# FFN stage: x plus its norm made by GpSimd from x alone, x (1 + rstd) - mean rstd, in one step with two per-row scalars (q's turn standing between k tile and q pair)

## The chip, the cores and the metric

The kernel runs on one core of a Trainium2 chip. The metric is the device time of one execution in microseconds (us). One execution was also recorded by the hardware profiler. The engines are TensorE (PE, with its weight loads as PEld), VectorE (DVE), ScalarE (ACT), GpSimd (POOL) and SyncE (SP, which issues DMAs here).

## The reference, cut to what matters

There are 16 blocks b of 128 rows by 1024 columns, float32. A cross attention makes the new x, and then the feed-forward part (FFN) follows:

```python
x = x + xattn(layernorm(x), ctx, ctx, ...)
h = layernorm(x)                 # (x - mean) / sqrt(var + 1e-5), over the 1024 columns
query  = h @ Wq.T                # 64 columns
scores = top 8 of 256 slots, softmax over them, weighted values, two small products -> aux_out
u      = log-variance term of h + sigmoid(gelu(h @ Wu1.T + bu1) @ Wu2.T + bu2)
gate   = sigmoid(gate_w1 * clip(u) + gate_bias)
x = x + (h + gate * aux_out)
```

The last line needs x + h. With rstd = 1/sqrt(var + eps) of a row, h = x rstd - mean rstd, so x + h = x (1 + rstd) - mean rstd.

## The kernel before, in words

All 16 blocks of x stay in SBUF as `X[:, b, :]` (`x_all` in the profile). No scheduler is at work: each engine has its own instruction stream, written out by hand as a loop over periods `b` with four quarters `i`, and the engines meet at counting semaphores (`wait_ge`). In periods 0 to 15 the attention of block b, b-1, b-2 and b-3 is interleaved: k tiles (`k_tile`), the q pair (`q_pair`), the turn of q (`q_turn`, between the k tile and the q pair), the context product (`g_part`), the output pair (`o_pair`), the turn of the output (`o_turn`).

FFN part 1 is a chain of 17 steps, `hidden_step(0)` to `hidden_step(16)`. Steps 0 to 7 stand in the quarters of periods 17 and 18, among the last attention work, the others behind them. In step b:

- ACT copies the turned block b+1 out of PSUM (`hT_high`, hT_hi), applies gelu to block b-1 (`unit_gelu`), makes the norm of block b+2 into one of two buffers (`h_scale`: `hbuf` from `X`), and sums the units of block b-1 (`unit_sum`). `o_copy` and `o_square` of the attention's last blocks stand between the steps.
- PE turns block b+1 (`h_transpose`, reads `hbuf`) and multiplies block b with the weights (`hidden_products`, 24 matmuls).
- DVE makes the low part of the turned block (`hT_low`), multiplies the gelu result by a row of weights (`unit_weights`: `units<-units,Wu`, both inputs in SBUF), and moves the products out of PSUM (`unit_bias`, `query_rows`).
- GpSimd adds the norm to x in place (`hidden_sum`: `X[b] = X[b] + hbuf`), which frees `hbuf` as far as GpSimd reads it. Its semaphore is `y_done`.

`h_scale(b)` writes `hbuf[:, b % 2, :]`. It waits for the norm's scalars (`nb2_done`), for PE to have turned block b-2 (`h_T`) and for GpSimd to have added block b-2 (`y_done`). The scalars come from `rstd2_pow(b)` on GpSimd, four small instructions on 128x1 tiles; `nb2` is -mean rstd. GpSimd's stream in periods 17 and 18 holds, in this order: `hidden_sum(0)`, the scaling of q for the last quarter, `rstd2_pow(13)`, `norm_scale(14)` (L977, L979, L981), `hidden_sum(1)` to `(3)`, `rstd2_pow(14)`, `hidden_sum(4)`, `norm_scale(15)`, `hidden_sum(5)` to `(7)`, `rstd2_pow(15)`, and then `hidden_sum(8)` to `(15)` with one other subtraction (L1062) in front of block 11. DVE uses the rstd of all blocks once, between its steps 7 and 8 (`varh`, L1330 and L1332, inputs in SBUF). `y_done` is also what part 2 waits for before it adds the gated term to `X[b]`.

FFN part 2 (from about 593 us) does the top 8, the softmax and the output products of the 16 blocks, and stores them.

Of the kernel before, what the change touches and what calls it, by code (L numbers as in the profile page):

```python
# [6 lines left out]
ALU = mybir.AluOpType  # L7
# [3 lines left out]
P = 128  # L11
B = 16
# [24 lines left out]
def wait(engine, sem, value):  # L37

    if value > 0:
        engine.wait_ge(sem, value)  # L40
# [7 lines left out]
def attention_ffn_kernel(nc, x, ctx_rows, ctx_cols, WqT_raw, WkT_raw, Wv_rows, WoT_rows, bo_row, g_col, Wuq_cols,  # L48
# [3 lines left out]
    with ctx:  # L52
        def sb(name, shape, dt=F32, scope=ctx):
            return scope.enter_context(nc.sbuf_tensor(name, shape, dt))

        def sem(name):
            return ctx.enter_context(nc.semaphore(name))


        X = sb("x_all", [P, B, N])  # L60
# [3 lines left out]
        mv2 = sb("mv2", [P, B, 2])  # L64
        rstd2 = sb("rstd2", [P, B, 1])
        nb2 = sb("nb2", [P, B, 1])
        VV = sb("VV", [P, NSLOT // P, P])
        scoreB = sb("scoreB", [P, 2 * NSLOT])

# [64 lines left out]
        hbuf = sb("hbuf", [P, 2, N], scope=ffn)  # L134
# [160 lines left out]
        ve2_done = sem("ve2_done")  # L295
        rstd2_done = sem("rstd2_done")
        mr2_done = sem("mr2_done")
        nb2_done = sem("nb2_done")

        wuq_hi = sem("wuq_hi")  # L300
# [9 lines left out]
        y_done = sem("y_done")  # L310
# [123 lines left out]
        def _(pe):  # L434
# [239 lines left out]
            def z_product(b, k):  # L674
                pe.wait_ge(wT_copied, b + 1)
                wait(pe, z_split, b)
                for s in range(NSLOT // P):
                    last = nc.tensor.matmul(z_psum, VV[:, s, :], wT[:, k, s, :], start=(s == 0),  # L678
                                            stop=(s == NSLOT // P - 1))
# [32 lines left out]
        def _(act):  # L712
# [64 lines left out]
            def h_scale(b, k):  # L777
                act.wait_ge(nb2_done, b + 1)
                wait(act, h_T, b - 1)
                wait(act, y_done, b - 1)  # L780
                nc.scalar.activation(hbuf[:, k, :], X[:, b, :], ACT.Identity, bias=nb2[:, b, :],
                                     scale=rstd2[:, b, :]).then_inc(h_done, 1)

# [14 lines left out]
            def hidden_step(b):  # L798
                if b + 1 < B:
                    hT_high(b + 1, (b + 1) % 2)  # L800
                if has(b - 1):
                    unit_gelu(b - 1, (b - 1) % 2)
                if b + 2 < B:
                    h_scale(b + 2, b % 2)
                if b == EARLY + 3:
                    act.wait_ge(varh_step, 2)
                    nc.scalar.activation(logv[:, :], varh[:, :], ACT.Ln, bias=ones[:, 0:1]).then_inc(logv_done, 1)
                if 0 < b < B:
                    unit_sum(b - 1, (b - 1) % 2)
# [14 lines left out]
            for b in range(PERIODS):  # L824
                p, o, e = b - 1, b - 2, b - 3
                for i in range(4):
# [6 lines left out]
                    if b == B + 1 and i == 0:  # L833
                        act.wait_ge(q_prod, 4 * B)
                        act.wait_ge(m_prod, B)
                        hT_high(0, 0)
                        h_scale(1, 1)
# [27 lines left out]
                    if b == 1 and i == 1:  # L865
                        act.wait_ge(vv_prod, NSLOT // P)
                        act.wait_ge(rk_prod, 1)
                        nc.scalar.copy(VV[:, :, :].rearrange("p s (r d) -> p s r d", d=VB),
                                       ob[:, 0:2 * VB].rearrange("p (s d) -> p s d", d=VB).unsqueeze(2).broadcast_to(
# [17 lines left out]
                    if b == B and i == 3:  # L887
                        for half in range(2):
                            act.wait_ge(k_moved[half], moved(B))
                        h_scale(0, 0)  # L890
# [49 lines left out]
        def _(pool):  # L940
# [43 lines left out]
            def rstd2_pow(b):  # L984
                pool.wait_ge(mv2_done, b + 1)
                nc.gpsimd.tensor_scalar(ve2[:, :], mv2[:, b, 1:2], LN_EPS, None, ALU.add).then_inc(ve2_done, 1)
                pool.wait_ge(ve2_done, b + 1)
                nc.gpsimd.tensor_tensor(rstd2[:, b, :], ve2[:, :], half_neg[:, 0:1], ALU.pow).then_inc(rstd2_done, 1)
                pool.wait_ge(rstd2_done, b + 1)
                nc.gpsimd.tensor_tensor(mr2[:, :], mv2[:, b, 0:1], rstd2[:, b, :], ALU.mult).then_inc(mr2_done, 1)  # L990
                pool.wait_ge(mr2_done, b + 1)
                nc.gpsimd.tensor_scalar(nb2[:, b, :], mr2[:, :], -1.0, None, ALU.mult).then_inc(nb2_done, 1)

            def hidden_sum(b):
                pool.wait_ge(h_done, b + 1)
                nc.gpsimd.tensor_tensor(X[:, b, :], X[:, b, :], hbuf[:, b % 2, :], ALU.add).then_inc(y_done, 1)

            nc.gpsimd.memset(half_neg[:, :], -0.5).then_inc(consts, 1)
            nc.gpsimd.memset(ones[:, :], 1.0).then_inc(consts, 1)
# [23 lines left out]
            for b in range(PERIODS):  # L1023
                p, o, e = b - 1, b - 2, b - 3
                for i in range(4):
                    if i == 0 and has(o):
                        mt_bias(o)
                    if i == 3 and 0 < b < B:
                        x_low(b)
                    if early_step(b, i) == 0:  # L1030
                        hidden_sum(0)
                    qb, qi = (p, i - 1) if i else (o, 3)
                    if has(qb):
                        q_scale(qb, qi)
                    if i == 0 and 0 < b < B:
                        rstd_pow(b)
                    if i == 0 and has(e - 1):
                        rstd2_pow(e - 1)
                    if i == 1 and b > 0 and has(b + 1):
                        ctx_low(b + 1)  # L1040
                    if i == 1 and has(e):
                        norm_scale(e)
                    if b == B and i == 3:
                        for half in range(2):
                            pool.wait_ge(k_moved[half], moved(B))
                        nc.gpsimd.memset(q_rows[:, :, BOT:P], 1.0).then_inc(query_ones, 1)
                    if early_step(b, i) > 0:
                        hidden_sum(early_step(b, i))
            rstd2_pow(B - 1)

            def output_scale(b):
# [6 lines left out]
            for b in range(EARLY, B):  # L1058
                hidden_sum(b)
                if b == EARLY + 2:  # L1060
                    pool.wait_ge(wvu_hi, 1)
                    nc.gpsimd.tensor_tensor(WvuT_lo[:, :], WvuT_in[:, :], WvuT_hi[:, :].bitcast(F32),  # L1062
                                            ALU.subtract).then_inc(wvu_lo, 1)
# [363 lines left out]
```

## Time and profile before

| | before |
|---|---|
| median of 3 runs | 643.58 us (642.69 to 644.58) |
| the profiled execution | 643.3 us |
| its span, first to last instruction | 641.4 us |
| mean granted TensorE clock | 0.997 of full speed |
| PE busy | 96% of the span |
| attention only, about 30.7 us a period | to about 500 us |
| steps of FFN part 1 | about 500 to 593 us |
| FFN part 2 | about 593 to 641 us |

The profiled execution lies 1.9 us over its span and 0.3 us under the median. "Busy" is the time in which an engine has an instruction running. Matmuls are pipelined: each row's duration reaches into the next one's, so the distance of two starts tells more than a duration.

### The profile page before, as it was taken

Reading aid. Unit: us, or ns where it says so; the run is one execution under the profiler, and the core shown is the slowest. Engines: PE = TensorE matmul, PEld = TensorE weight load, DVE = VectorE, ACT = ScalarE, POOL = GpSimd, SP = SyncE. Lnnn points to the kernel's source line nnn. Section 1 sums busy time; section 2 is a strip of 40 time slices with the busy share of each in tenths; the row PEclk is TensorE's granted clock in tenths of the full one; section 3 lists DMA queues with packets and bytes.
Section 4 is the critical chain, followed back from the end, with each engine's and each line's share of the span. In section 5 each row is a group of like instructions: output and inputs, shape, how many; then the busy total and the mean of one; then the engine's idle time right before and its main releaser. Section 6 shows DMA issues by size and latency. Waiting matters only on the chain.

```text
span 641.4 us, 11774 instructions
## 1 busy us (share of the span) xinstructions
PE 617.7 (96%) x3974; PEld 542.3 (85%) x3974; DVE 546.0 (85%) x757; ACT 416.7 (65%) x844; POOL 387.1 (60%) x353
## 2 busy tenths in 40 slices
PE   4899999999999999999999999999999989999896
PEld 3778888888888888888898888888888989988574
DVE  5989898988989898989898989898986745866896
ACT  5566766676676666667676766675665856674793
POOL 4954474747474747474747565665745668662394
PEclk9999999999999999999999999999999999999899
DMA  8933443444444444444445343443343100000056
GB/s 297 248 107 102 142 110 117 117 127 113 126 115 121 114 129 115 126 115 122 125 116 161 100 129 103 132 107 94 80 145 96 42 2 1 1 2 1 34 228 263
DMA packets 52010, 72.57 MB, mean 113 GB/s; under 512 B 10112, under 2 KB 42400, under 8 KB 51696
## 3 DMA queue, kind: packets, MB, share of 16 engines
q1 hardware_dynamic: 50912, 68.07, 36.3%
q0 software_dynamic: 896, 2.45, 1.2%
q10 hardware_dynamic: 144, 1.31, 0.6%
q8 instruction: 32, 0.52, 0.4%
q14 instruction: 26, 0.21, 0.1%
HBM read 29.85 MB, written 8.39 MB: 60 GB/s over the span
## 4 chain that ended last, share of the span: by engine, by line
PE 86%; DVE 4%; POOL 2%; ACT 2%; issue 2%; SPq 2%; DMA 1%; DVEq 0%; ACTq 0%
PE ob L502 17%; PE gm L479 17%; PE turn L463 8%; PE k_slot L437 5%; PE q_slot L437 5%; PE q_slot L439 4%; PE k_slot L439 4%; PE k_slot L438 4%; PE q_slot L438 4%; PE turn L554 3%; PE gm L488 2%; PE turn L510 2%; PE gm L554 2%; SPq L381 2%; PE turn L678 1%
## 5 line engine op out<-in xcount | busy, mean ns | idle before, releaser
L966 POOL TENSOR_TENSOR qs_sb<-qs_sb,qrec 128x1024 f32<-128x1024 f32 x64 | 122.0, 1906 | 151.2 <-DVE qrec L1131 151.2
L734 ACT ACTIVATE ek<-k_slot,nkm 128x1024 f32<-128x1024 f32 x62 | 69.1, 1114 | 95.5 <-DVE nkm L1096 95.4
L502 PE MATMUL ob<-mt_sb,q_hd 128*128 128x128 f32 x1024 | 126.4, 277 | 1.9 <-ACT o_sb L756 1.8
L502 PEld LDWEIGHTS ob<-mt_sb,q_hd 128*128 128x128 f32 x1024 | 121.8, 192 | 6.4 <-issue 4.8
L479 PE MATMUL gm<-ekT,ctxT 128*128 128x256 f32 x512 | 118.2, 379 | 0.9 <-DMA ekT<-kt 0.9
L479 PEld LDWEIGHTS gm<-ekT,ctxT 128*128 128x128 f32 x512 | 97.0, 190 | 15.9 <-DMA ekT<-kt 1.4
L744 ACT ACTIVATE qs_sb<-qs_sb 128x1024 f32<-128x1024 f32 x64 | 68.6, 1071 | 31.6 <-DVE qs_sb L1120 31.6
L1096 DVE TENSOR_REDUCE nkm<-k_slot 128x1 f32<-128x1024 f32 x62 | 74.2, 1197 | 16.1 <-PE k_slot L439 16.1
L1127 DVE TENSOR_REDUCE qsum<-qs_sb 128x16 f32<-128x1024 f32 x64 | 76.9, 1202 | 4.1 <-ACT qs_sb L744 4.1
L1120 DVE TENSOR_TENSOR qs_sb<-q_slot,qm 128x1024 f32<-128x1024 f32 x64 | 78.4, 1225 | 2.2
L1103 DVE STREAM_TRANSPOSE kt<-ek 128x1024 f32<-128x1024 f32 x64 | 78.5, 1227 | 0.0
L1117 DVE TENSOR_REDUCE qm<-q_slot 128x16 f32<-128x1024 f32 x64 | 75.5, 1180 | 0.0
L463 PE MATMUL turn<-ident,qs_sb 128*128 128x128 f32 x512 | 66.3, 272 | 0.0
L463 PEld LDWEIGHTS turn<-ident,qs_sb 128*128 128x128 f32 x512 | 59.6, 141 | 8.0 <-issue 0.5
L749 ACT COPY q_hd<-turn 128x1024 f32<-128x1024 f32 x64 | 64.3, 1005 | 2.9 <-PE turn L463 2.9
L437 PE MATMUL k_slot<-ctx_hi,WkT_hi 128*128 128x512 f32 x124 | 54.8, 442 | 9.5 <-DVE ctx_lo L1281 7.5
L437 PE MATMUL q_slot<-WqT_hi,xn_hi 128*128 128x512 f32 x128 | 55.7, 435 | 0.0
L439 PE MATMUL q_slot<-WqT_lo,xn_hi 128*128 128x512 f32 x128 | 50.6, 395 | 0.0
L438 PE MATMUL q_slot<-WqT_hi,xn_lo 128*128 128x512 f32 x128 | 49.8, 389 | 0.0
L439 PE MATMUL k_slot<-ctx_lo,WkT_hi 128*128 128x512 f32 x124 | 49.3, 398 | 0.0
L438 PE MATMUL k_slot<-ctx_hi,WkT_lo 128*128 128x512 f32 x124 | 49.0, 395 | 0.0
L960 POOL TENSOR_TENSOR xn_lo<-xn,xn_hi 128x1024 fp32r<-128x1024 f32 x16 | 38.3, 2392 | 14.9 <-ACT xn_hi L728 14.9
(199 smaller groups left out, 1250.8 us busy)
## 6 DMA issues: line engine op xcount, KB each, us to landing
ekT<-kt SPq DMA_DIRECT2D x496, 64.0 KB, 2.0
ctx_in<-ctx_rows SPq DMA_DIRECT2D x16, 512.0 KB, 4.6
x_all<-x SPq DMA_DIRECT2D x16, 512.0 KB, 3.5
ctxT<-ctx_cols SPq DMA_DIRECT2D x16, 512.0 KB, 4.1
out<-q_hd SPq DMA_DIRECT2D x15, 512.0 KB, 2.6
Wuq_in<-Wuq_cols ACTq DMA_DIRECT2D x1, 1280.0 KB, 6.3
x_all<-values_cols POOLq DMA_DIRECT2D x1, 1024.0 KB, 8.1
ekT<-kt POOLq DMA_DIRECT2D x16, 64.0 KB, 3.6
```

The source lines that it names most:

```text
L437: nc.tensor.matmul(dst, lhs[0], rhs[0], start=True, stop=False)
L438: nc.tensor.matmul(dst, lhs[1], rhs[0], start=False, stop=False)
L439: return nc.tensor.matmul(dst, lhs[0], rhs[1], start=False, stop=True)
L463: last = nc.tensor.transpose(turn[:, (2 * t + n) * P:(2 * t + n + 1) * P], qs_sb[:, i % 2, n * HALF + t * P:n * HALF + (t + 1) * P], ident ...
L479: last = nc.tensor.matmul(gm[:, cols], ctxT[:, b % 2, j, :], ekT[:, 2 * half:2 * half + 2, :, j * BLK:(j + 1) * BLK], start=(j == 0), stop ...
L502: last = nc.tensor.matmul(ob[:, (j % 4) * C:(j % 4 + 1) * C], q_hd[:, t, j * P:(j + 1) * P], mt_sb[:, b % 2, t, :], start=(t == 0), stop=( ...
L966: nc.gpsimd.tensor_tensor(e, e, qrec[:, i % 2, :].unsqueeze(2).broadcast_to([P, PAIR, DH]), ALU.mult).then_inc(q_mul, 1)
L1096: V.tensor_reduce(nkm[:, i:i + 1], k_psum(b, i)[:, :], AX, ALU.max, negate=True).then_inc(k_max, 1)
L1103: V.transpose(kt[:, i, :], ek[:, i % 2, :]).then_inc(k_T, 1)
L1117: V.tensor_reduce(qm[:, :], q, AX, ALU.max).then_inc(q_max, 1)
L1120: V.tensor_tensor(qs_sb[:, i % 2, :].rearrange("p (m d) -> p m d", d=DH), q, qm[:, :].unsqueeze(2).broadcast_to([P, PAIR, DH]), ALU.subtra ...
L1127: V.tensor_reduce(qsum[:, :], qs_sb[:, i % 2, :].rearrange("p (m d) -> p m d", d=DH), AX, ALU.add).then_inc(q_sum, 1)
```

## The change

Three things are edited. GpSimd's `hidden_sum` reads `X` alone and applies two per-row scalars, a multiply by `one_rstd2` and an add of `nb2`, in one instruction. The scalar `one_rstd2` = 1 + rstd is one further small GpSimd instruction in `rstd2_pow`. ACT's `h_scale` no longer waits for `y_done`. `hidden_sum(b)` still waits for `h_done`, since it overwrites `X[b]`, which `h_scale(b)` reads.

```diff
@@ h_scale (ACT) @@
                 act.wait_ge(nb2_done, b + 1)
                 wait(act, h_T, b - 1)
-                wait(act, y_done, b - 1)
                 nc.scalar.activation(hbuf[:, k, :], X[:, b, :], ACT.Identity, bias=nb2[:, b, :],
                                      scale=rstd2[:, b, :]).then_inc(h_done, 1)
@@ rstd2_pow and hidden_sum (GpSimd) @@
                 nc.gpsimd.tensor_scalar(nb2[:, b, :], mr2[:, :], -1.0, None, ALU.mult).then_inc(nb2_done, 1)
+                nc.gpsimd.tensor_scalar(one_rstd2[:, b, :], rstd2[:, b, :], 1.0, None, ALU.add).then_inc(one_rstd2_done, 1)
 
             def hidden_sum(b):
                 pool.wait_ge(h_done, b + 1)
-                nc.gpsimd.tensor_tensor(X[:, b, :], X[:, b, :], hbuf[:, b % 2, :], ALU.add).then_inc(y_done, 1)
+                pool.wait_ge(nb2_done, b + 1)
+                pool.wait_ge(one_rstd2_done, b + 1)
+                nc.gpsimd.tensor_scalar(X[:, b, :], X[:, b, :], one_rstd2[:, b, :], nb2[:, b, :], ALU.mult,
+                                        ALU.add).then_inc(y_done, 1)
```

GpSimd's stream in period 17, from `rstd2_pow(13)` to the start of `rstd2_pow(14)`, before (`rstd` and `nb` are rstd2 and nb2, names without their numbers):

```order
L992 TENSOR_SCALAR nb<-mr 128x1 [waits mr2_done]
L977 TENSOR_SCALAR l2c<-l 128x8 [waits l2_sum]
L979 TENSOR_TENSOR rn<-l2c,half_neg 128x8 [waits l2_clamped]
L981 TENSOR_TENSOR o_sb<-o_sb,rn 128x1024 [waits rn_pow]
L996 TENSOR_TENSOR x_all<-x_all,hbuf 128x1024 [waits h_done] x3
L986 TENSOR_SCALAR ve<-mv 128x1 [waits mv2_done]
```

and the same place of the changed kernel, whose lines have other numbers:

```order
L993 TENSOR_SCALAR nb<-mr 128x1 [waits mr2_done]
L994 TENSOR_SCALAR one_rstd<-rstd 128x1
L978 TENSOR_SCALAR l2c<-l 128x8 [waits l2_sum]
L980 TENSOR_TENSOR rn<-l2c,half_neg 128x8 [waits l2_clamped]
L982 TENSOR_TENSOR o_sb<-o_sb,rn 128x1024 [waits rn_pow]
L1001 TENSOR_SCALAR x_all<-x_all,one_rstd,nb 128x1024 [waits one_rstd2_done,nb2_done,h_done] x3
L987 TENSOR_SCALAR ve<-mv 128x1 [waits mv2_done]
```

Nothing changes its place: one small instruction is put in, and the three sums are another instruction with more waits.

ACT's stream in step 1, from gelu(0) to the copy of block 15's first output half (`o_copy`), before:

```order
L791 ACTIVATE units<-units 128x256 [waits units_biased]
L781 ACTIVATE hbuf<-x_all,nb,rstd 128x1024 [waits y_done,h_T,nb2_done]
L795 ACTIVATE units,learned<-units 128x256 [waits gelu_weighted]
L756 COPY o_sb<-ob 128x512 [waits l2_sum,o_T,o_prod]
L787 CAST hT_hi<-q_slot 128x1024 [waits units_prod,h_T]
```

and now:

```order
L792 ACTIVATE units<-units 128x256 [waits units_biased]
L782 ACTIVATE hbuf<-x_all,nb,rstd 128x1024 [waits h_T,nb2_done]
L796 ACTIVATE units,learned<-units 128x256 [waits gelu_weighted]
L758 COPY o_sb<-ob 128x512 [waits l2_sum,o_T,o_prod]
L788 CAST hT_hi<-q_slot 128x1024 [waits units_prod,h_T]
```

The order is the same, and the one wait is gone. PE's and DVE's streams are the same but for line numbers.

## Rows read from the trace of the kernel before

**Rows 1.** The page: busy us (share of the span) xinstructions of each engine.
```profile
PE 617.7 (96%) x3974; PEld 542.3 (85%) x3974; DVE 546.0 (85%) x757; ACT 416.7 (65%) x844; POOL 387.1 (60%) x353
```

**Rows 2.** Waits: engine line <- waited for: us in total, times, longest.
```profile
ACT units L795 <- DVE units L1166: 10.6, 11, 3.1
...
ACT hbuf L781 <- POOL x_all L996: 3.0, 2, 1.9
```

**Rows 3.** Timeline of ACT: start us, us, instruction, idle before and releaser.
```profile
516.67 0.42 ACT L791 ACTIVATE units<-units 128x256 f32<-128x256 f32 x1
518.24 1.24 ACT L781 ACTIVATE hbuf<-x_all,nb,rstd 128x1024 f32<-128x1024 f32 x1 [1.16 <-POOL x_all L996]
519.39 0.40 ACT L795 ACTIVATE units<-units 128x256 f32<-128x256 f32 x1
...
519.78 0.56 ACT L756 COPY o_sb<-ob 128x512 f32<-128x512 f32 x1
...
542.21 1.24 ACT L781 ACTIVATE hbuf<-x_all,nb,rstd 128x1024 f32<-128x1024 f32 x1 [1.86 <-POOL x_all L996]
```

**Rows 4.** Timeline of PE at the three places where it waits.
```profile
517.65 1.04 PE L510 MATMUL turn<-ident,o_sb 128*128 128x128 f32 x8
520.49 2.02 PE L502 MATMUL ob<-mt_sb,q_hd 128*128 128x128 f32 x16 [1.80 <-ACT o_sb L756]
...
537.28 0.31 PE L554 MATMUL gm<-WuqT_lo,hT_hi 128*128 128x320 f32 x1
537.90 1.09 PE L541 MATMUL k_slot<-ident,hbuf 128*128 128x128 f32 x8 [0.31 <-ACT hbuf L781]
...
542.35 1.04 PE L510 MATMUL turn<-ident,o_sb 128*128 128x128 f32 x8
543.51 1.09 PE L541 MATMUL q_slot<-ident,hbuf 128*128 128x128 f32 x8
...
561.29 0.27 PE L561 MATMUL gm<-ident,q_rows 128*128 128x128 f32 x1
561.40 0.27 PE L561 MATMUL ob<-ident,q_rows 128*128 128x128 f32 x1
562.01 1.09 PE L541 MATMUL q_slot<-ident,hbuf 128*128 128x128 f32 x8 [0.33 <-ACT hbuf L781]
```

**Rows 5.** Timeline of DVE: instructions with two inputs in SBUF.
```profile
517.12 1.29 DVE L1166 TENSOR_TENSOR units<-units,Wu 128x256 f32<-128x256 f32 x1 [0.51 <-ACT units L791]
...
525.61 0.41 DVE L1166 TENSOR_TENSOR units<-units,Wu 128x256 f32<-128x256 f32 x1
...
531.80 1.37 DVE L1166 TENSOR_TENSOR units<-units,Wu 128x256 f32<-128x256 f32 x1
...
554.15 2.31 DVE L1332 TENSOR_TENSOR varh<-varh,rstd 128x16 f32<-128x16 f32 x1
556.39 1.21 DVE L1149 TENSOR_TENSOR hT_lo<-q_slot,hT_hi 128x1024 fp32r<-128x1024 f32 x1
557.52 1.54 DVE L1166 TENSOR_TENSOR units<-units,Wu 128x256 f32<-128x256 f32 x1
```

**Rows 6.** Timeline of GpSimd: the sums, and the small operations of rstd2_pow(14).
```profile
515.73 7.21 POOL L996 TENSOR_TENSOR x_all<-x_all,hbuf 128x1024 f32<-128x1024 f32 x3
529.03 0.23 POOL L986 TENSOR_SCALAR ve<-mv 128x1 f32<-128x1 f32 x1 [6.10 <-DVE mv L1144]
...
530.47 2.42 POOL L996 TENSOR_TENSOR x_all<-x_all,hbuf 128x1024 f32<-128x1024 f32 x1
...
551.70 7.07 POOL L996 TENSOR_TENSOR x_all<-x_all,hbuf 128x1024 f32<-128x1024 f32 x3
```

**Rows 7.** Groups of GpSimd's instructions by form: xcount, busy us, mean ns, idle before.
```profile
L992 POOL TENSOR_SCALAR nb<-mr 128x1 f32<-128x1 f32 x16 | 3.8, 236 | 1.4
...
L1046 POOL MEMSET q_rows<- 128x1024 f32 x1 | 1.0, 953 | 0.0
```

**Rows 8.** Timeline of GpSimd in an attention period, behind rstd2_pow.
```profile
303.77 1.92 POOL L966 TENSOR_TENSOR qs_sb<-qs_sb,qrec 128x1024 f32<-128x1024 f32 x1 [2.40 <-DVE qrec L1131]
```

More of the change, by code:

```diff
@@ L66, in attention_ffn_kernel @@
         nb2 = sb("nb2", [P, B, 1])
+        one_rstd2 = sb("one_rstd2", [P, B, 1])
         VV = sb("VV", [P, NSLOT // P, P])
@@ L297, in attention_ffn_kernel @@
         mr2_done = sem("mr2_done")
+        one_rstd2_done = sem("one_rstd2_done")
         nb2_done = sem("nb2_done")
```

## The prediction

> **What bounds the kernel now.** I read the page first: PE is busy in 96% of the span, GpSimd in 60% [rows 1]. So GpSimd's own time is worth nothing by itself. What counts is where PE waits for something that GpSimd or ACT gives late. The list of waits, read next, has two entries for the place of the change: ACT waits for GpSimd's sum before it may write `hbuf`, 3.0 us in two pieces, and ACT waits 10.6 us in 11 pieces for DVE's `unit_weights` (L1166) [rows 2]. Then I read the timelines of the FFN steps, to see which of these waits reach PE. There are three places.
>
> *Place 1.* ACT's gelu(0) ends at 517.09, but the norm of block 3 starts at 518.24, behind the first of three sums. `unit_sum` and `o_copy` stand behind it in ACT's stream [rows 3]. PE is idle for 1.80 us until that copy has come, and starts at 520.49 [rows 4].
>
> *Place 2.* The second of ACT's two waits ends at 542.21, and `hbuf` of block 7 is there at 543.45 [rows 3]. PE turns it at 543.51. The turn before it started at 542.35 [rows 4], and eight transposes take about 8 x 0.11 = 0.87 us from start to start (0.11 is the distance of the two rows before 562.01). So PE lost 543.51 - 543.22 = 0.29 us. Block 6's turn, at 537.90, also came late: the last matmul before it started at 537.28, these follow each other by 0.15, so 0.47 us were lost [rows 4].
>
> *Place 3.* At 562.01 PE waited for `hbuf` of block 11. The transpose before it started at 561.40, so 562.01 - 561.51 = 0.50 us were lost [rows 4].
>
> Places 2 and 3 are made by something that no wait list names. `unit_weights` on DVE takes 0.41 us at 525.61, but 1.29, 1.37 and 1.54 us at 517.12, 531.80 and 557.52. `varh`, 16 columns, takes 2.31 us [rows 5]. Each long one lies under a GpSimd sum and ends just behind one: 518.41 behind the first third of 515.73 + 7.21 (518.13); 533.17 behind 530.47 + 2.42 = 532.89; 556.46 behind two thirds of 551.70 + 7.07 (556.41); 559.06 behind all of it (558.77) [rows 5, 6]. So a DVE operation with two inputs in SBUF stands still until the running sum is over, and the sum's length is on PE's path although GpSimd has time.
>
> **The change, part by part.**
>
> *The wait that ACT loses* is gone whatever the new instruction costs. In place 1 the norm of block 3 can start behind gelu(0), at about 517.0, which is 1.25 us earlier (the 1.16 of wait and 0.09 by which ACT's rows overlap) [rows 3]. For that to reach PE, `unit_sum(0)` must not wait for DVE instead: it stood at 519.39 and would now stand at 518.14, so `unit_weights(0)` must be over by then.
>
> *The sum's new price d.* The trace has no GpSimd operation with one 128x1024 tensor in, one out and two scalars. From below: a memset of 128x1024, which only writes, takes 0.95 us [rows 7]. From above: the sum now, two tensors in, takes 2.42 [rows 6]. One read and one write are nearer to the memset if reads and writes go side by side, and halfway if the software loop counts. I take 1.2, and keep 0.95 and 2.42 as ends. I don't exclude a price above 2.42 (the instruction has two arithmetic steps): that is the slow rival below. The Trainium skill (GPSIMD Engine Reference, 3.1) gives about 1.8 cycles an element at 1.2 GHz for a tight one-input loop, an estimate of 1.5 us; no run here shows it, and the sum below would come out the same by it.
>
> *The added small instruction* is like L992: 0.24 us [rows 7] and about 0.08 between two, 0.33 in all, 16 times. In the attention periods GpSimd waits 2.40 us for DVE behind `rstd2_pow` [rows 8], so it costs nothing; without this cover it would be 13 x 0.33 = 4.3 us. In period 17 it pushes `norm_scale(14)` and the sums back by 0.33: block 14's turn on PE at 517.65 needs data that were there at 515.8 [rows 4, 6], so 1.9 us of cover are left. The two added waits stand behind a wait for ACT that comes later than both, since ACT itself waits for the same scalar; behind them in GpSimd's queue are only further sums.
>
> *Place 1 with d = 1.2.* First sum 516.06 to 517.26. `unit_weights(0)` wants to start at 517.12, stands until 517.26 and needs 0.29 more, as now: over at 517.55, in time for 518.14. So PE's start moves by the whole 1.25 us, to 519.24; it was free at 518.69.
>
> *Place 2.* All is now 1.25 earlier. `rstd2_pow(14)` starts at 527.78 instead of 529.03, the sum behind it at 529.55 (1.44 of small operations as now [rows 6], and 0.33), over at 530.75. `unit_weights(2)` wants to start at 530.55 (531.80 - 1.25), so it is over at about 531.05 instead of 533.17, 2.1 earlier. ACT follows by the same amount, and block 6's `hbuf` is there about 0.3 us before PE wants it: the 0.47 is won. Block 7's `hbuf` no longer waits at all: 0.29 more. Next late thing: DVE's copies of the products, which fit under each turn as they do in the steps between.
>
> *Place 3.* `varh` and the following `unit_weights` meet at most one short sum each in place of a whole 2.36. hT_lo of block 9, at 556.39 now [rows 5], keeps only PE's distance, and ACT is about 1 us ahead of PE's turn of block 11: 0.50 won.
>
> *Transposes that start behind a wait* take 1.09 instead of 1.04 [rows 4]: 0.05 to 0.06 for each of three that no longer wait, 0.15.
>
> Sum: 1.25 + 0.47 + 0.29 + 0.50 + 0.15 = 2.66, say 2.7 us. Everything behind 563 us follows PE's stream, and nothing there starts by a clock of its own. The profiled execution took 643.3 us, so 640.6; it lies 0.3 under the median of the runs shown, so the forecast for a median is **640.9 us**. By my bound, 0.3% or 1.9 us (about what a measurement of this kernel tells from no change), this is faster.
>
> **How the sum depends on d.** Up to about 1.5 us it stays: each long DVE operation still ends before ACT or PE asks for it. At 1.9, `unit_weights(0)` is over at 516.06 + 1.9 + 0.29 = 518.25, so place 1 gives 1.1; place 2 still gives its two terms less 0.2; in all about 2.3. At 2.42 place 1 gives 0.6, because the sum starts 0.33 later than now. In place 2 `unit_weights(2)` is over only 0.3 earlier, and DVE cuts the gain back to that; block 7 brings 0.3 more; in place 3 three sums in a row start 0.3 before they do now, DVE again is released only 0.3 earlier, and about 0.3 us is left in all.
>
> **Rivals.**
>
> *A. The sum isn't shorter (d from 2.0 to 2.7).* For it: GpSimd's time could go by steps of a software loop and not by tensors read. Against it: the memset's 0.95. The time is 643.3 - 0.3 = 643.0, for a median 643.3.
>
> *B. Only half of place 1.* The waiting DVE operation may be passed over by the next sum, since sums 2 and 3 are already queued. The Trainium skill (SBUF — State Buffer, "SBUF: two separate sides") states that the port pair is an exclusive lock, and that "whichever [...] starts first gets the pair for the whole instruction". By this rule a sum that is issued first would go first. The row at 517.12 speaks against it: three sums were queued back to back, and DVE got in behind the first [rows 5, 6]. If it lost its turn at 517.26, it would be over at 518.46 + 0.29 = 518.75, place 1 would give 0.6, and the total is 2.0: 641.6 for a median.
>
> *C. Slower: the new instruction is dear.* One mechanism: at d = 3.0 `unit_weights(0)` is over at 519.35 and place 1 gives nothing. In place 2 the sum runs from 530.8 to 533.8, `unit_weights(2)` is over at 534.1 instead of 533.17, and PE loses 0.9 (0.6 behind block 7). In place 3 the three sums end at 561.6 instead of 558.8, and DVE and PE lose 2.8: 643.3 + 2.8 = 646.1, for a median 646.4. It decides by 0.3% from d = 2.8, and is even at 2.5. For it: two arithmetic steps with scalars read from memory, in software. Against it: small operations of this kind cost 0.24, and two steps on the same data need not double that [rows 7].
>
> *D. The gain doesn't arrive.* Part 2 could take it back, if DVE or the stores end last there. PE is idle more there, but each of its inputs comes from PE's own products of part 1. About 1 to 2 us would be left: 642.
>
> **Chances.** Forecast (d up to 1.9, gain 2.1 to 3.0) 0.66; A 0.14; B 0.07; C 0.06; D 0.07. Faster by over 0.3%: the forecast and half of B, 0.69. Slower: C, with a little left at A's upper end, 0.06. Same: 0.25. The forecast's own range is 640.4 to 641.5. The range for 8 in 10 goes from 640.0 (all of the forecast, with 0.6 for what rounding and small gaps on PE may give) to 643.4, which takes in A and D.
>
> **What would show it.** In the profile of the changed kernel: the sum's mean duration, 1.2 (1 to 1.9 would do); no L1166 above about 1 us, and a `varh` below 1.5; no wait of ACT for a sum; PE's gap behind block 14's turn 0.5 instead of 1.8; the attention periods still 30.7 us. I am wrong if the sum takes over 2 us, if DVE operations stay long under short sums, or if a gap on PE grows between 563 and 641.

## The result and the profile after

| | before | changed kernel |
|---|---|---|
| median of 5 runs each | 643.58 us (642.55 to 644.58) | 640.41 us (640.05 to 641.01) |
| ratio of the two | | 0.9944 (95%: 0.9919 to 0.9970) |
| the profiled execution | 643.3 us | 640.05 us |
| its span | 641.4 us | 638.1 us |
| mean granted TensorE clock | 0.997 | 0.999 |

The change made the kernel faster, by 3.2 us between the medians of this comparison, against 2.7 forecast. The ratio in the table is an estimate over all the runs, and not the quotient of the two medians, which is 0.9951; its interval stands for gains from 1.9 to 5.2 us. In a second comparison, told below, it was 1.2 us between the medians. The trace says what belongs to the change, and the clock of the runs accounts for a good part of what differs between the two comparisons.

The page of the changed kernel, busy time of each engine:

```profile
PE 615.7 (96%) x3974; PEld 541.3 (85%) x3974; DVE 540.2 (85%) x757; ACT 416.9 (65%) x844; POOL 371.7 (58%) x369
```

GpSimd has 16 more instructions and 15 us less to do, DVE 6 us less with the same instructions [rows 1]. The groups of GpSimd's instructions, one for each shape (busy us, mean ns | idle before):

```profile
L1001 POOL TENSOR_SCALAR x_all<-x_all,one_rstd,nb 128x1024 f32<-128x1024 f32 x16 | 19.7, 1236 | 16.1 <-ACT hbuf L782 16.1
L994 POOL TENSOR_SCALAR one_rstd<-rstd 128x1 f32<-128x1 f32 x16 | 3.4, 213 | 0.0
```

The price that no row of before showed is 1.24 us in the mean, three in a row take 3.73 to 3.81. The new small instruction is 0.21. Waits of the changed kernel:

```profile
POOL x_all L1001 <- ACT hbuf L782: 16.1, 5, 4.8
...
ACT units L796 <- DVE units L1172: 6.9, 12, 3.0
...
PE ob L504 <- ACT o_sb L758: 0.5, 1, 0.5
```

ACT's wait for a sum (3.0 us, [rows 2]) is gone, and its wait for `unit_weights` fell from 10.6 to 6.9. ACT's timeline in step 1, which answers to [rows 3]:

```profile
516.61 0.42 ACT L792 ACTIVATE units<-units 128x256 f32<-128x256 f32 x1
516.93 1.24 ACT L782 ACTIVATE hbuf<-x_all,nb,rstd 128x1024 f32<-128x1024 f32 x1
518.06 0.40 ACT L796 ACTIVATE units<-units 128x256 f32<-128x256 f32 x1
...
518.46 0.56 ACT L758 COPY o_sb<-ob 128x512 f32<-128x512 f32 x1
```

PE's timeline at the places of [rows 4], and the first product of part 2's scores:

```profile
517.59 1.03 PE L512 MATMUL turn<-ident,o_sb 128*128 128x128 f32 x8
519.17 2.02 PE L504 MATMUL ob<-mt_sb,q_hd 128*128 128x128 f32 x16 [0.54 <-ACT o_sb L758]
...
536.10 1.04 PE L543 MATMUL k_slot<-ident,hbuf 128*128 128x128 f32 x8
540.61 1.03 PE L512 MATMUL turn<-ident,o_sb 128*128 128x128 f32 x8
541.48 1.04 PE L543 MATMUL q_slot<-ident,hbuf 128*128 128x128 f32 x8
...
559.36 1.04 PE L543 MATMUL q_slot<-ident,hbuf 128*128 128x128 f32 x8
...
589.20 1.02 PE L569 MATMUL gm<-scoreB,query 128*128 128x512 f32 x2
```

The last one in the trace of before:

```profile
591.90 1.02 PE L567 MATMUL gm<-scoreB,query 128*128 128x512 f32 x2
```

Block 14's turn (L510, L512) starts at 517.65 before and at 517.59 now, so the attention stage gave nothing. Taken from that turn, the starts are:

| PE starts, us behind block 14's turn | before | after | won | forecast |
|---|---|---|---|---|
| first product of the output pair | 2.84 | 1.58 | 1.26 | 1.25 |
| block 6's turn | 20.25 | 18.51 | 1.74 | 1.72 |
| block 7's turn | 25.86 | 23.89 | 1.97 | 2.06 |
| block 11's turn | 44.36 | 41.77 | 2.59 | 2.61 |
| first score product of part 2 | 74.25 | 71.61 | 2.64 | 2.66 |

(The forecast column adds up the prediction's terms, with 0.05 for each transpose that starts without a wait.) The FFN steps gave 2.64 us. DVE in the changed kernel follows. The rows at 517.05, 530.47, 551.42 and 553.63 answer to those of [rows 5] with 1.29, 1.37, 2.31 and 1.54; the 0.73 and 0.88 are two further `unit_weights` that still meet a short sum:

```profile
517.05 0.48 DVE L1172 TENSOR_TENSOR units<-units,Wu 128x256 f32<-128x256 f32 x1 [0.51 <-ACT units L792]
...
530.47 0.41 DVE L1172 TENSOR_TENSOR units<-units,Wu 128x256 f32<-128x256 f32 x1
...
539.37 0.73 DVE L1172 TENSOR_TENSOR units<-units,Wu 128x256 f32<-128x256 f32 x1
...
551.22 0.17 DVE L1336 TENSOR_TENSOR varh<-mv,rstd 128x16 f32<-128x16 f32 x1
551.42 1.07 DVE L1338 TENSOR_TENSOR varh<-varh,rstd 128x16 f32<-128x16 f32 x1
...
553.63 0.42 DVE L1172 TENSOR_TENSOR units<-units,Wu 128x256 f32<-128x256 f32 x1
...
558.02 0.88 DVE L1172 TENSOR_TENSOR units<-units,Wu 128x256 f32<-128x256 f32 x1
```

**Where the remaining 0.7 us of the spans' 3.3 is.** 0.06 of it lies ahead of block 14's turn, and 0.6 behind the first score product: 641.4 - 591.90 = 49.5 us before, 638.1 - 589.20 = 48.9 after. The first stretch of part 2, by windows (start:end, us, busy time of PE, PEld, DVE, ACT, POOL with instructions, granted clock, DMA share, GB/s), before:

```profile
592.10:600.00 7.90, 5.34 (x17) 2.97 (x16) 6.87 (x26) 5.30 (x15) 0.00 (x0) 0.78 0.00 0
600.00:641.40 41.40, 35.09 (x175) 25.31 (x173) 34.88 (x103) 28.39 (x67) 29.46 (x20) 0.99 0.51 203
```

after:

```profile
589.40:597.30 7.90, 4.60 (x20) 2.36 (x19) 7.07 (x27) 5.26 (x15) 0.00 (x0) 1.00 0.00 0
597.30:638.10 40.80, 34.66 (x172) 24.93 (x170) 34.63 (x103) 28.38 (x67) 29.50 (x20) 0.99 0.51 206
```

and in another execution of the same changed kernel (the second comparison's):

```profile
588.94:596.84 7.90, 5.32 (x19) 2.34 (x18) 6.87 (x27) 5.27 (x15) 0.00 (x0) 0.88 0.00 0
596.84:638.60 41.76, 35.58 (x174) 26.04 (x173) 34.92 (x104) 28.34 (x67) 29.54 (x20) 0.95 0.50 202
```

In all three executions PE had just been idle for 2.10 us; the row of the last one is:

```profile
593.14 0.41 PE L672 MATMUL turn<-ident,w_sb 128*128 128x128 f32 x2 [2.10 <-issue]
```

The granted clock then fell in two executions of three, to a mean of 0.78 and of 0.88 over the window, that is to its lower level (1.2 GHz) for a part of it. The first score product behind the idle stretch shows it, 1.71 us before and 1.02 in the changed kernel's first trace:

```profile
598.41 1.71 PE L567 MATMUL gm<-scoreB,query 128*128 128x512 f32 x2
```
```profile
595.04 1.02 PE L569 MATMUL gm<-scoreB,query 128*128 128x512 f32 x2
```

The traces of all the runs below settle whether the change has a part in this. With those of before and of the changed kernel's first run there are twelve, and PE is idle for the same 2.10 us in each. In six of them that product takes 1.02, and part 2, from its first score product (589.20 above) to the end of the span, takes 48.8 to 49.1 us. They are the changed kernel's first trace, the kernel without sums, those with sums of 1.93, 2.42 and 2.96 us, and the first with the copy moved early. In the other six it takes 1.71 to 1.92, and part 2 takes 49.4 to 49.7 us: before, the changed kernel's second trace (49.7), the old wait, the old sum without the wait, the five small ones, and the second with the copy moved early. Two kernels that were traced twice stand on both sides, and kernels with long sums stand on the short side. So the 0.6 us goes by whether the clock fell in the traced execution. Whether the change has an influence on how often it falls, twelve traces don't show.

### The profile page after: what moved, and what is told of

The parts are those of the page before. It is cut to its first block, busy times and chain, and to the rows that moved or that the text cites. A ratio compares the mean times of both kernels' runs of the same rounds, so it can differ in the third digit from the quotient of the medians.

```text
span 638.1 us, 11806 instructions
## 1 busy us (share of the span) xinstructions
PE 615.7 (96%) x3974; PEld 541.3 (85%) x3974; DVE 540.2 (85%) x757; ACT 416.9 (65%) x844; POOL 371.7 (58%) x369
## 4 chain that ended last, share of the span: by engine, by line
PE 92%; DVE 3%; SPq 2%; issue 1%; ACT 1%; DMA 1%; DVEq 0%; ACTq 0%
PE ob L504 18%; PE gm L481 17%; PE turn L465 8%; PE k_slot L439 5%; PE q_slot L439 5%; PE k_slot L441 5%; PE q_slot L441 4%; PE gm L556 4%; PE k_slot L440 4%; PE q_slot L440 4%; PE turn L556 4%; PE gm L490 2%; PE turn L512 2%; SPq L383 2%; PE turn L680 1%
## 5 line engine op out<-in xcount | busy, mean ns | idle before, releaser
L504 PE MATMUL ob<-mt_sb,q_hd 128*128 128x128 f32 x1024 | 126.4, 277 | 0.6 <-ACT o_sb L758 0.5
L504 PEld LDWEIGHTS ob<-mt_sb,q_hd 128*128 128x128 f32 x1024 | 121.8, 192 | 5.2 <-issue 3.6
```

The costliest lines, as they stand in the source:

```text
L504: last = nc.tensor.matmul(ob[:, (j % 4) * C:(j % 4 + 1) * C], q_hd[:, t, j * P:(j + 1) * P], mt_sb[:, b % 2, t, :], start=(t == 0), stop=( ...
```

## The experiments

Ten runs were made in three sets, each with its own runs of before on the same chip (medians 643.64, 643.58 and 643.41). Beside the times stands what the trace says free of part 2's spread: the distance from the start of block 14's turn on PE to the first score product, 74.25 us before.

| run | distance | won by it | median | below its before | ratio (95%) |
|---|---|---|---|---|---|
| changed kernel, first trace | 71.61 | 2.64 | 640.41 | 3.17 | 0.9944 (0.9919 to 0.9970) |
| changed kernel, again | 71.60 | 2.65 | 642.24 | 1.17 | 0.9967 (0.9950 to 0.9984) |
| old wait put back | 71.90 | 2.35 | 641.07 | 2.57 | 0.9958 (0.9943 to 0.9973) |
| old sum, no wait | 73.02 | 1.23 | 642.39 | 1.25 | 0.9990 (0.9975 to 1.0005) |
| no sums at all | 71.62 | 2.63 | 640.35 | 3.29 | 0.9958 (0.9943 to 0.9973) |
| sum of 1.93 us | 71.75 | 2.50 | 641.31 | 2.33 | 0.9966 (0.9953 to 0.9980) |
| sum of 2.42 us | 73.82 | 0.43 | 642.93 | 0.65 | 0.9995 (0.9979 to 1.0010) |
| sum of 2.96 us | 76.63 | -2.38 | 645.70 | -2.12 | 1.0034 (1.0021 to 1.0046) |
| before, five small ones | 76.78 | -2.53 | 645.97 | -2.39 | 1.0042 (1.0027 to 1.0056) |
| copy moved early | 70.84 | 3.41 | 639.83 | 3.75 | 0.9939 (0.9924 to 0.9955) |
| copy moved early, again | 70.83 | 3.42 | 640.06 | 3.35 | 0.9941 (0.9923 to 0.9959) |

The distance repeats to 0.01 us between two executions of one kernel (there are two such pairs); the medians follow it within 0.3 us in seven of the eleven rows and within 0.7 in three more. The second run of the changed kernel is off by 1.5 and is taken up last. The intervals of "old sum, no wait" and "sum of 2.42 us" take in 1, and those of the versions near the changed kernel overlap one another: between these it is the distance that tells, not the medians.

**1. The wait alone.** The changed kernel, with ACT's wait for the sum put back:

```diff
                 wait(act, h_T, b - 1)
+                wait(act, y_done, b - 1)
                 nc.scalar.activation(hbuf[:, k, :], X[:, b, :], ACT.Identity, bias=nb2[:, b, :],
```

> The changed kernel with ACT's wait for the sum put back (the one-input sum stays). Theory (the length of GpSimd's sum holds up DVE and ACT; the wait is worth little once the sum is short): block 3's norm starts behind the first of three sums, at about 517.2 instead of 516.93, so PE's gap before block 15's third output quarter grows by 0.27 us and nothing else moves: 640.4 + 0.3 = 640.7 us. Rival (the removed wait is what gained): back to about 643.3 us.

ACT's timeline of this kernel, and its PE:

```profile
519.07 1.25 ACT L783 ACTIVATE hbuf<-x_all,nb,rstd 128x1024 f32<-128x1024 f32 x1 [0.19 <-POOL x_all L1002]
```
```profile
519.44 1.04 PE L512 MATMUL turn<-ident,o_sb 128*128 128x128 f32 x8
521.33 0.91 PE L504 MATMUL ob<-mt_sb,q_hd 128*128 128x128 f32 x6 [0.85 <-ACT o_sb L758]
```

From L512 to L504 it is 1.89 us instead of 1.58, so the wait costs 0.31 once the sum is short. With a 1.2 us sum the wait is nearly over by itself: most of the gain is the sum's length, not the wait taken away.

**2. The other half: the old sum, without the wait.** The kernel before, where a third buffer (`xn`, free by then) lets the norm of block b go ahead of the sum of block b-2:

```diff
+        hb = [hbuf[:, 0, :], hbuf[:, 1, :], xn[:, :]]
...
-                wait(act, y_done, b - 1)
-                nc.scalar.activation(hbuf[:, k, :], X[:, b, :], ACT.Identity, bias=nb2[:, b, :],
+                wait(act, y_done, b - 2)
...
+                nc.scalar.activation(hb[b % 3], X[:, b, :], ACT.Identity, bias=nb2[:, b, :],
```

> The kernel before, with its two-input sum of 2.4 us, but a third buffer for the norm (xn, dead by then), so that ACT waits only for the sum one block further back, which is long over. Theory: place 1 gains 0.95 us (DVE's unit_weights(0) still stands until 518.4), the block 6 gap on PE (0.47) stays, block 7's 0.29 is won, the stretch of varh and three sums stays: 643.6 - 1.3 = 642.3 us. Rival 1 (the wait is all): 640.7. Rival 2 (the sum's length is all): 643.6.

PE of this kernel:

```profile
517.77 1.03 PE L511 MATMUL turn<-ident,o_sb 128*128 128x128 f32 x8
519.68 1.58 PE L503 MATMUL ob<-mt_sb,q_hd 128*128 128x128 f32 x12 [0.88 <-ACT o_sb L757]
```

The gap is 1.91 us, 0.93 less than before (forecast 0.95) and not 1.26, since `unit_weights(0)` still stands until the old sum is over (1.29 us, as before). Blocks 6 and 11 still wait. It gave 1.2 us in all: the wait without the shorter sum is less than half.

**3. The sum's length.** Four kernels differ from the changed one in the sum alone. One puts a 128x1 operation in its place, one adds X to itself (one tensor read twice), one adds a block of weights to X (two tensors), one works on 1280 columns of the weights. The first and the last leave x's update out altogether, the other two add X or the weights in place of the norm.

```diff
-                nc.gpsimd.tensor_scalar(X[:, b, :], X[:, b, :], one_rstd2[:, b, :], nb2[:, b, :], ALU.mult,
-                                        ALU.add).then_inc(y_done, 1)
+                nc.gpsimd.tensor_scalar(tiny[:, b:b + 1], one_rstd2[:, b, :], 1.0, None, ALU.mult).then_inc(y_done, 1)
...
+                nc.gpsimd.tensor_tensor(X[:, b, :], X[:, b, :], X[:, b, :], ALU.add).then_inc(y_done, 1)
...
+                nc.gpsimd.tensor_tensor(X[:, b, :], X[:, b, :],
+                                        Wuq_in[:, :, :].rearrange("p j c -> p (j c)")[:, 0:N], ALU.add).then_inc(y_done, 1)
...
+                wait(pool, y_done, b)
+                nc.gpsimd.tensor_tensor(flat[:, 0:1280], flat[:, 0:1280], flat[:, 1280:2560], ALU.add).then_inc(y_done, 1)
```

> The changed kernel without the sums: GpSimd does a 128x1 operation in the place of each, so the output lacks x's own update by the norm. Theory: what DVE still waits for sums in the changed kernel (unit_weights 0.48, 0.73 and 0.88 us, varh 1.07) is off PE's path, so the time is that of the changed kernel within 0.1 us in the trace: 640.4 us. Rival (sums of 1.2 us still cost something on the path, or GpSimd's reads slow other engines): 639.9 or less.

> The changed kernel with the sum made as x + x by an operation with two tensor inputs, so the FFN's residual is left wrong: it leaves out the norm. No wait on ACT, the small instruction stays, only the length of the sum goes back to about 2.4 us. Theory: place 1 gives 0.6, block 6's gap stays, three sums hold up varh and unit_weights(7) as before, 0.3 us of gain left in all: 643.3 us; PE waits again for hbuf of blocks 6 and 11. Rival (ACT's wait was what mattered): 640.7.

> The changed kernel with the sum made from two different tensors (x and a block of weights in place of the norm, so x's own update is left wrong), since x + x took only 1.93 us. Length 2.4 us, no wait on ACT, small instruction kept. Theory: place 1 gives 0.6, block 6's gap on PE comes back, hbuf of block 11 is late again, 0.3 us of gain in all: 643.3 us. Rival (ACT's wait was what mattered): 641.3 or less, as at 1.93 us.

> The changed kernel with a GpSimd operation of 1280 columns and two different inputs in the place of each sum, 3.0 us long (x's own update is left out). Theory: place 1 gives nothing, unit_weights(2) is over 0.9 us later than in the kernel before, the three sums before block 11 end 2.8 us later: 646.4 us, so slower than before although ACT waits for no sum. Rival (GpSimd has time enough, only its waits count): 641 to 643.

Without sums the distance is 71.62, the same as with the 1.24 us sums: these cost nothing any more. DVE of the kernel without sums has `varh` at 0.17 twice:

```profile
551.30 0.17 DVE L1336 TENSOR_TENSOR varh<-mv,rstd 128x16 f32<-128x16 f32 x1
551.50 0.17 DVE L1338 TENSOR_TENSOR varh<-varh,rstd 128x16 f32<-128x16 f32 x1
```

The groups of the other three show what their sums took:

```profile
L1001 POOL TENSOR_TENSOR x_all<-x_all 128x1024 f32<-128x1024 f32 x16 | 30.7, 1929 | 10.9 <-ACT hbuf L782 10.9
```
```profile
L1003 POOL TENSOR_TENSOR x_all<-x_all,Wuq_in 128x1024 f32<-128x1024 f32 x16 | 38.5, 2424 | 8.6 <-ACT hbuf L782 8.6
```
```profile
L1005 POOL TENSOR_TENSOR Wuq_in<-Wuq_in 128x1280 f32<-128x1280 f32 x16 | 47.3, 2957 | 6.6 <-ACT hbuf L782 5.5 <-POOL Wuq_in L1005 1.0
```

The second kernel missed its expectation, which took 2.4 us for X + X: it took 1.93, and what came is near the prediction's value for 1.9 us (2.3 us won, 641.3): 2.5 by the distance, 2.3 by the medians. The kernel with two tensors was made to have the missing point. PE and DVE of it, at 2.42 us:

```profile
517.18 1.03 PE L512 MATMUL turn<-ident,o_sb 128*128 128x128 f32 x8
519.30 2.02 PE L504 MATMUL ob<-mt_sb,q_hd 128*128 128x128 f32 x16 [1.08 <-ACT o_sb L758]
...
536.88 1.09 PE L543 MATMUL k_slot<-ident,hbuf 128*128 128x128 f32 x8 [0.35 <-ACT hbuf L782]
...
561.11 1.09 PE L543 MATMUL q_slot<-ident,hbuf 128*128 128x128 f32 x8 [0.32 <-ACT hbuf L782]
```
```profile
516.64 1.50 DVE L1174 TENSOR_TENSOR units<-units,Wu 128x256 f32<-128x256 f32 x1 [0.51 <-ACT units L792]
...
530.60 1.55 DVE L1174 TENSOR_TENSOR units<-units,Wu 128x256 f32<-128x256 f32 x1
...
553.24 2.34 DVE L1340 TENSOR_TENSOR varh<-varh,rstd 128x16 f32<-128x16 f32 x1
```

The long DVE operations are back, and with them PE's three waits; 0.43 us of the gain is left (the prediction had 0.3). At 2.96 us the kernel is slower than before, by 2.4 us of distance (the prediction had 2.8 for 3.0). PE waits at block 6, among the products between the turns of blocks 8 and 9, and in front of block 12's turn. DVE's longest row under the sums stands behind them:

```profile
538.80 1.09 PE L543 MATMUL k_slot<-ident,hbuf 128*128 128x128 f32 x8 [0.36 <-ACT hbuf L782]
...
550.70 0.38 PE L556 MATMUL gm<-WuqT_hi,hT_hi 128*128 128x320 f32 x1 [1.14 <-DVE q_rows L1167]
...
569.37 1.09 PE L543 MATMUL k_slot<-ident,hbuf 128*128 128x128 f32 x8 [0.47 <-ACT hbuf L782]
```
```profile
547.39 2.70 DVE L1175 TENSOR_TENSOR units<-units,Wu 128x256 f32<-128x256 f32 x1
```

Rival C's mechanism and size hold, its places do not. Laid beside the changed kernel's starts on PE, this one loses 1.0 us in place 1 (2.63 behind the turn instead of 1.58), 1.2 in front of block 6's turn, 1.3 in front of block 9's and 1.5 in front of block 12's, 5.0 in all (76.63 - 71.61). The one in front of block 9 is the wait of 1.14 for `q_rows`, which stands behind the `unit_weights` of 2.70 us in DVE's stream. Rival C had the whole loss of 2.8 against the kernel before on PE by block 11's turn. There it was 0.9 us; at block 12's turn it was 2.3.

**4. Work on GpSimd where it has no cover.** The kernel before, with five further 128x1 operations behind `rstd2_pow`:

```diff
+                for n in range(5):
+                    nc.gpsimd.tensor_scalar(extra[:, n:n + 1], rstd2[:, b, :], 1.0, None, ALU.add).then_inc(extra_done, 1)
```

> The kernel before with five more 128x1 operations behind each of GpSimd's rstd2_pow, about 0.2 us each, 1.0 in all. Theory: nothing in the attention periods (30.7 us still, GpSimd waits 2.4 us there), but 1.0 us at each of the three places of the FFN steps, because the sums behind them start later and DVE waits for their ends: 643.6 + 3 = 646.6 us. Rival 1 (covered everywhere): 643.6. Rival 2 (they cost in each attention period too): over 650.

GpSimd of it in an attention period:

```profile
301.09 0.88 POOL L997 TENSOR_SCALAR extra<-rstd 128x1 f32<-128x1 f32 x5
303.51 1.92 POOL L968 TENSOR_TENSOR qs_sb<-qs_sb,qrec 128x1024 f32<-128x1024 f32 x1 [1.54 <-DVE qrec L1136]
```

The wait that stood at 2.40 [rows 8] is 1.54, and the period is unchanged (30.74 us in both): 0.9 us of work cost nothing there. In the FFN steps the same five cost 2.5 us, because they push back the sums that DVE and ACT wait behind. The expectation had 1.0 at each of the three places, 3 us in all. They came as 0.84 in place 1, 0.83 at block 6 and 0.87 at block 11, which is the 0.88 that the five take, three times. PE's gap in place 1, 1.80 before [rows 4], is now:

```profile
521.40 0.79 PE L504 MATMUL ob<-mt_sb,q_hd 128*128 128x128 f32 x5 [2.65 <-ACT o_sb L758]
```

(The changed kernel's one small instruction leaves 2.23 us of this wait.)

**5. What is late next.** The gap of 0.54 that is left in place 1 is ACT's `o_copy`, which stands behind the norm and `unit_sum`. Put ahead of the step for the last block:

```diff
-                    if i == 2 and has(o):
+                    if i == 2 and has(o) and o < B - 1:
                         o_copy(o, 0)
...
+                    if i == 1 and o == B - 1:
+                        o_copy(o, 0)
```

> The changed kernel with ACT's copy of block 15's first output half moved ahead of step 1, where ACT waits 1.65 us for PE. Theory: PE's gap behind block 14's turn (0.54, and the 0.17 that a start behind a wait costs) closes and everything behind follows: 640.4 - 0.7 = 639.7 us. Rival (another input is late there or in block 11, or ACT's later work moves back): 640.4.

```profile
518.04 1.04 PE L512 MATMUL turn<-ident,o_sb 128*128 128x128 f32 x8
518.92 1.95 PE L504 MATMUL ob<-mt_sb,q_hd 128*128 128x128 f32 x16
```

PE starts 0.88 behind the turn instead of 1.58, as soon as the turn is over, and 0.77 of the distance is won. By the medians this version is faster than before in both of its runs; against the changed kernel the ratios' intervals overlap, and the distance says that it is shorter. It was run again, together with the changed kernel:

> The kernel with the copy ahead of step 1 again, beside the changed kernel on the same chip. Theory: 0.6 to 0.7 us less than the changed kernel at equal mean clock, 639.4 us at 0.999. Rival: no difference.

> The changed kernel again, to compare executions of equal mean clock. Before, executions at a mean clock of 0.999 took 642.7 us in the middle, those at 0.993 to 0.996 some 1.8 us more. Theory (2.7 us come from the FFN steps, the rest of the measured 3.2 from which executions fell where): at 0.999 it takes 640.0 to 640.3, and the difference of the medians at equal clock is 2.5 to 2.8 us. Rival (the change gains more than the three places, in part 2 too): 3.1 us or more at equal clock, and a part 2 of the trace that is shorter at equal clock.

It gave 640.06, the changed kernel 642.24. The distances, 70.83 and 71.60, are those of the first time. The expectation had 0.6 to 0.7 less than the changed kernel at equal clock, 639.4 at 0.999. One run had that clock, with 639.77, and two had 0.995, with 640.06 and 640.07 beside 640.41 of the changed kernel: too few to tell 0.4 from 0.7.

**The changed kernel's 640.4 and 642.2.** Each run lists its granted clock, and the time goes with it. Medians at equal clock, with the changed kernel's 14 runs and the 66 runs of before from the three sets:

| mean clock | before (runs) | changed (runs) | difference |
|---|---|---|---|
| 0.999 | 642.77 (22) | 640.15 (4) | 2.6 |
| 0.996 | 644.72 (10) | 642.24 (1) | 2.5 |
| 0.995 | 643.62 (16) | 640.41 (5) | 3.2 |
| 0.993 | 646.23 (4) | 642.62 (3) | 3.6 |

(One run of the changed kernel, 642.76, was at 0.992, and 14 of before at 0.994, 0.997 and 1.0.) The first five runs of the changed kernel were at 0.995 and 0.999 alone; of the nine later ones five were at 0.992 to 0.996 and over 642.2. At equal clock the change is worth 2.6 and 3.2 us in the two rows with four and five of its runs, and 2.5 and 3.6 in those with one and three. The trace's 2.64 lies within them. The expectation for the second run of the changed kernel was 2.5 to 2.8 at equal clock, and its rival had 3.1 or more with a shorter part 2. So the first came at 0.999 and at 0.996, the rival's number at 0.995 and 0.993. The rival's other sign did not come: part 2 of that trace took 49.7 us, and by the twelve traces above its length goes by the clock.

Part 2 is not the only stage that differs. Block 14's turn starts anywhere from 517.18 to 519.44 us in the twelve traces. In the latest of them, that of the old wait, the mean granted clock was 0.97 over the first 60 us, and 1.00 in the changed kernel's first trace, where the turn starts at 517.59. The distance leaves both ends out, and the medians have them in.

## Why the mechanism was right, and the step that failed, point by point

- **What bounds.** Right. PE's three places, and the DVE operations that stand under a sum as the hidden cause of two of them, are what changed.
- **The sum's price, 1.2.** Measured 1.24, much nearer to the lower bound of 0.95 than to 2.42. That 1.2 was so close is partly luck: no row decided between the memset's price and halfway. The Trainium skill (GPSIMD Engine Reference, 3.1) has about 1.8 cycles an element as the best case, for a tight loop without branching on data, and by it the sum would take an estimated 1.5 us. The trace has less, 1.24 x 1200 / 1024 = 1.45 cycles at the same 1.2 GHz. For two tensors the Trainium skill has about 2.6 cycles there, and the row with 2424 ns gives 2.84.
- **Place 1, 1.25.** Measured 1.26, with `unit_weights(0)` at 0.48 as against 1.29. The two experiments on the halves part it: the old wait brings 0.31 back; the old sum without the wait wins 0.93.
- **Places 2 and 3, and the transposes.** The forecast 2.66 came as 2.64. Block 7's turn had 0.09 less than forecast, and block 11's step made up 0.07 of it. `varh` met one sum (1.07), within the bound of 1.5.
- **The small instruction at nothing.** Right in the attention (2.23 us of wait left), and right in period 17 as far as the totals tell; with five of them it is not free there.
- **"Everything behind 563 us follows PE's stream, and nothing there starts by a clock of its own."** This is the step that failed: it put part 2 at nothing. Part 2 took 49.5 us in the trace of before and 48.9 in that of the changed kernel, 0.6 us beside the 2.66 of the sum. Over twelve traces it took 48.8 to 49.1 us or 49.4 to 49.7, by whether the granted clock fell behind PE's idle stretch of 2.10 us. The stages up to block 14's turn had a spread too, 2.3 us over the twelve, and the prediction carried one profiled execution over to a median with nothing for either. So the medians' difference, 3.17, lies above the sum's 2.66 and outside the 2.1 to 3.0 that the forecast gave the gain, and the ratio 0.9944 stands for 3.6 us, while in the second comparison the medians differed by 1.17. What the change itself gives, 2.64, was forecast well.
- **The range.** Its numbers don't follow from one another. A gain of 3.0 gives 640.6 and not 640.4, and 0.6 below the forecast 640.9 is 640.3; the 640.0 comes out only if 0.6 is taken from the profiled execution's 640.6. The median 640.41 lies 0.4 inside the range for 8 in 10, which is less than the 0.6 by which part 2 differs, so that it does is luck in part.
- **How it depends on d.** The forecast for other lengths held at 1.93 (2.3 forecast, 2.5 measured), at 2.42 (0.3, 0.43) and at 2.96 (about -2.8, -2.4). It is even at about 2.5, by a line between the last two.
- **Rivals.** A didn't come: d wasn't in 2.0 to 2.7. B, that DVE loses its turn to a queued sum, is refuted by the row at 517.05: it began 1.15 us into the first of three queued sums and took 0.48. The three took 3.81 from 515.90, so behind the second it would have been over only at 518.44 + 0.29, after 1.7 us. The Trainium skill (SBUF — State Buffer, "SBUF: two separate sides") calls the shared port pair an exclusive lock, and that a DVE operation blocks until the sum is over is what the rows of 1.5 to 2.7 us show; who goes first of two that wait, the rows settle for DVE. C needed a price that the instruction hasn't, and the run at 2.96 us shows that its mechanism is real, though its places were others. D didn't come: the distance to part 2 kept all of it, and no gap grew between 563 and 589.

Open: what decides whether an execution's clock falls after the idle stretch in part 2, and whether the differences at equal clock, 2.5 to 3.6, differ by more than chance.

## What to carry to other kernels

A GpSimd instruction can lie on TensorE's path although GpSimd is 60% busy and the wait lists name it only in part: look for VectorE operations with two SBUF inputs whose duration varies, and lay their ends beside the ends of GpSimd's long instructions. Then the length of one GpSimd instruction is what counts, not its sum, and halving it (one tensor and two per-row scalars in place of two tensors) was worth more here than taking a wait away (2.35 us against 1.23). Once it ends before anyone asks, making it shorter still gives nothing: 1.24 us and none at all were the same here.

For differences below one per cent, compare the distance of two starts on the bounding engine. It repeated to 0.01 us where the changed kernel's medians, of five and of nine runs, moved by 1.8. It sees only the stages between the two starts, so the rest has to be laid beside it, as for part 2 here.

## What the runs showed of the hardware

- GpSimd, float32, 128x1024: one tensor with two per-row scalars 1.24 us, X + X 1.93, two different tensors 2.42. So the same tensor read twice is cheaper than two, and it isn't the arithmetic that costs: two steps in the cheapest, one in the dearest.
- A VectorE operation of 16 columns, 0.17 us alone, takes 1.07 under a short sum and 2.34 under a long one. The stall goes by GpSimd's instruction, not by its own size.
- A VectorE operation that waited got in before the next queued GpSimd instruction, with three back to back: 0.48 us in all from 517.05, in a block of three that took 3.81.
- After the same 2.10 us of idle time of TensorE the granted clock stayed at its upper level in six traces of twelve and fell for a part of the next stretch in the other six, two kernels being in both groups. Means over the next 7.9 us were 1.00, 0.88 and 0.78 in three of them. From the first score product to the end of the span it took 48.8 to 49.1 us in the first six and 49.4 to 49.7 in the others.
